# Causal attention: values projected per group of four heads in three rotating buffers, ten exponential slots in place of eight

## The chip, the cores and the metric

The kernel runs on one core of a Trainium2 chip. The metric is the device time of one execution in microseconds (us); the median of three runs of the kernel before is 2347.75 us (2345.16 to 2347.81). The engines are TensorE (PE in the profile, PEld for its weight loads), VectorE (DVE), ScalarE (ACT), GpSimd (POOL) and SyncE (SP, which here issues the DMAs).

## What is computed

A decoder layer for 4 batch elements of 1024 tokens and 512 channels: causal self-attention with 16 heads of 32 channels, cross-attention to 64 context tokens, a feed-forward part, and then a gated fusion that ends in a layer norm. All of it is float32. The change lies in the causal self-attention:

```python
xn1 = _ln(x, g1, be1)
q = jnp.einsum('btc,hcd->bhtd', xn, Wq) + bq[None, :, None, :]
k = jnp.einsum('bsc,hcd->bhsd', kv_src, Wk) + bk[None, :, None, :]
v = jnp.einsum('bsc,hcd->bhsd', kv_src, Wv) + bv[None, :, None, :]
scores = jnp.einsum('bhtd,bhsd->bhts', q, k) / scale      # scale = DH ** -0.5, so this multiplies
scores = jnp.where(mask[None, None], scores, -jnp.inf)
attn = jax.nn.softmax(scores, axis=-1)
out = jnp.einsum('bhts,bhsd->bhtd', attn, v)
```

## The kernel before, in words

The program has three stages: causal attention (1), cross-attention (2), feed-forward and fusion (3). Stage 1 runs over 16 groups g: batch element b = g // 4, four heads each. A group has two halves c2 (queries 0 to 511 and 512 to 1023); a half goes over key tiles j of 128 keys, 4 in the first half and 8 in the second, and over the four heads i.

The order of the work is written out by hand as a table of planned times: `order1` gives each step a number (1 unit is one group), sorts them, and every engine then walks the same list and takes the steps that are its own. An engine's queue is in order. `banks1` gives each step that needs PSUM one of seven banks, the eighth (`BO`) collects the attention output.

The steps that the change and the prediction touch:

- `lnT`, `lnh`, `lnl`: the layer norm of a batch element, transposed by PE (L722), split into a high part (`Q.xh`, ACT) and a low part (`Q.xl`, DVE). For b > 0 these stand in the third group of the batch element before.
- `pj`: projection of queries and keys of a group, `three` matmuls per k (L55, L56, L57: high by high, high by low, low by high), 512 columns each.
- `vm` and `ve`: projection of the values. One `vm` step is one k of one token tile st: `three` matmuls whose stationary operand is `Q.xh` or `Q.xl` (128 channels by 128 tokens) and whose moving operand is the whole row of `Wv`, 512 columns, so all 16 heads. Four k fill one PSUM bank, which `ve` (ACT, L873) copies to `Q.v[:, st, :]`. There are 8 st per batch element. For b = 0 they stand in the part ahead of group 0; for b > 0 in the second half of the last group of batch element b - 1, and `ve` waits until that group has read `Q.v[:, st, :]` for the last time (`s_pv`).
- `mx` (L745, DVE L1000 and L1004): the row maxima, from a matmul of their own.
- `sc` (L785), `low` (DVE L1011, the causal mask), `ex` (ACT L895): scores with keys on the partitions, and their exponentials. Tile j = 0 of a half goes to `Q.esum`, all others to a ring `Q.er` of 8 slots, `at % 8`. An `ex` waits until POOL has added the slot's former content into `esum` (`s_add`) and PE has multiplied it by the values (`s_pv`).
- `pv` (PE L797): four matmuls of exponentials by values, 32 output rows each, and on POOL the four additions into `esum` (L660). `fin` (L806) sums over the keys, `sao` (ACT L902) evicts the attention output of a half.

```python
def three(e, dst, lhs, rhs, start, stop):
    (lh, ll), (rh, rl) = lhs, rhs
    e.matmul(dst, lh, rh, start=start, stop=False)
    e.matmul(dst, lh, rl, start=False, stop=False)
    return e.matmul(dst, ll, rh, start=False, stop=stop)
```

`Q.v` is a tile of 8 rows of 512 elements per partition. Ahead of group 0 the same tile holds the tokens of batch element 0 (`x_rows`).

## Time and profile before

| | |
|---|---|
| median of three runs | 2347.75 us (2345.16 to 2347.81) |
| profiled execution | span 2338.9 us from the first to the last instruction |
| what lies around the span | 8.85 us, from the span to the median of the runs |
| stage 1, groups 0 to 15 | about 116 to 1033 us of the span |
| PE matmul / weight loads busy | 94% / 68% of the span |
| DVE / ACT / POOL busy | 60% / 37% / 40% of the span |

No time of the profiled execution beyond its span is listed, so the median stands for it. A matmul in the trace lasts longer than the distance to the next one, since matmuls are pipelined: what a matmul costs is read from start to start. A "busy" PE can still be waiting inside; idle time of PE is a lower bound on what it lacks.

### The profile page before, as it was taken

The page shows a single profiled execution, that of the slowest core. Times are in us where ns is not written, and L with a number is a line of the kernel's source. Part 1 is how long each engine was busy: PE and PEld are TensorE (multiplying, and loading weights), DVE is VectorE, ACT ScalarE, POOL GpSimd, SP SyncE. Part 2 cuts the span into 40 slices and gives each one's busy share as a digit, 9 for nine tenths or more (in the row PEclk, how much of TensorE's full clock was granted, in tenths as well). Part 3 has the DMA queues.
Part 4 walks back from the last instruction along what each step waited for, and adds up shares of the span by engine and source line. Part 5 has one row for each costly group of instructions (what it writes and reads, how often), then busy time and mean ns, then how long its engine had stood idle before and what let it go on. Part 6 is the DMA issues. An engine that isn't in the chain of part 4 may idle for free.

```text
span 2338.9 us, 31417 instructions
## 1 busy us (share of the span) xinstructions
PE 2198.0 (94%) x11206; PEld 1595.5 (68%) x11206; DVE 1410.1 (60%) x3349; ACT 868.2 (37%) x1598; POOL 933.6 (40%) x943
## 2 busy tenths in 40 slices
PE   7999999999999998789999998999999999999996
PEld 5655565556555654447777776788887887888784
DVE  5477757875786566735666668453455546454646
ACT  3155545654565455533443334321111122112213
POOL 1068657766777577773333333010111202011212
PEclk9999999999999998789999999999999999999998
DMA  7465545553556356212111121321112121212011
GB/s 231 55 93 97 92 71 77 103 93 62 83 97 97 60 88 124 69 56 85 59 55 55 59 95 55 113 86 36 50 54 75 52 82 44 87 55 68 33 36 50
DMA packets 106320, 177.29 MB, mean 76 GB/s; under 512 B 18334, under 2 KB 23454, under 8 KB 106160
## 3 DMA queue, kind: packets, MB, share of 16 engines
q1 hardware_dynamic: 106164, 175.29, 32.4%
q8 instruction: 88, 1.44, 0.3%
q14 instruction: 68, 0.56, 0.1%
HBM read 83.67 MB, written 40.13 MB: 53 GB/s over the span
## 4 chain that ended last, share of the span: by engine, by line
PE 75%; DVE 9%; issue 6%; ACT 4%; POOL 3%; DMA 2%; SPq 0%; POOLq 0%; ACTq 0%; DVEq 0%
PE psum L55 18%; PE psum L56 17%; PE psum L57 17%; PE psum L797 5%; PE psum L745 5%; PE psum L785 4%; PE psum L806 2%; DMA small<-es 2%; PE psum L703 1%; DVE psum L1000 1%; POOL es L660 1%; ACT sx L1346 1%; PE psum L1300 1%; DVE mx L1004 1%; PE psum L1292 1%
## 5 line engine op out<-in xcount | busy, mean ns | idle before, releaser
L660 POOL TENSOR_TENSOR es<-es,er 128x512 f32<-128x512 f32 (+3 forms) x640 | 589.6, 961 | 322.5 <-PE psum L797 283.4
L895 ACT ACTIVATE er<-psum 128x512 f32<-128x512 f32 (+3 forms) x640 | 280.4, 470 | 316.0 <-DVE psum L1011 181.2
L1000 DVE CUSTOM_DVE_ANT_0 psum<-psum,mask_ts 128x384 f32<-128x384 f32 (+3 forms) x512 | 247.9, 500 | 201.2 <-PE psum L745 200.5
L785 PE MATMUL psum<-qs,ks 100*128 100x512 f32 (+3 forms) x768 | 264.5, 377 | 17.1 <-DVE mx L1004 6.6
L745 PE MATMUL psum<-ks,qs 96*128 96x512 f32 (+3 forms) x768 | 267.2, 373 | 10.9 <-DVE mx L1000 6.6
L1850 ACT ACTIVATE fy<-psum,cols 128x512 f32<-128x512 f32 x128 | 88.2, 689 | 451.4 <-PE psum L57 450.9
L745 PEld LDWEIGHTS psum<-ks,qs 96*128 96x128 f32 x768 | 144.0, 194 | 109.7 <-issue 39.4
L1004 DVE TENSOR_REDUCE mx<-psum 128x1 fp32r<-128x512 f32 x256 | 175.1, 684 | 60.7 <-PE psum L745 59.8
L785 PEld LDWEIGHTS psum<-qs,ks 100*128 100x128 f32 x768 | 145.9, 196 | 92.4 <-DVE mx L1004 23.1
L55 PE MATMUL psum<-fh,hh 128*128 128x512 f32 x512 | 201.1, 393 | 7.1 <-DVE hl L1951 7.1
L55 PE MATMUL psum<-fah,fh 128*128 128x512 f32 x512 | 202.6, 396 | 0.0
L57 PE MATMUL psum<-fah,fl 128*128 128x512 f32 x512 | 199.8, 390 | 0.0
L56 PE MATMUL psum<-fal,fh 128*128 128x512 f32 x512 | 199.6, 390 | 0.0
L57 PE MATMUL psum<-fh,hl 128*128 128x512 f32 x512 | 199.4, 389 | 0.0
L56 PE MATMUL psum<-fl,hh 128*128 128x512 f32 x512 | 199.3, 389 | 0.0
L1949 DVE CAST hh<-fy 128x512 fp32r<-128x512 f32 x128 | 59.5, 465 | 228.8 <-ACT fy L1850 228.4
L1215 POOL TENSOR_TENSOR pp<-pp,small 128x1024 f32<-128x1024 f32 x32 | 61.2, 1913 | 266.7 <-DVE small L1481 266.7
L797 PE MATMUL psum<-er,v 128*32 128x512 f32 (+3 forms) x1280 | 152.3, 497 | 6.7 <-ACT er L895 6.2
L1746 POOL TENSOR_TENSOR et<-et,vpb 128x512 f32<-128x512 f32 x24 | 35.4, 1476 | 284.8 <-ACT et L1876 284.8
L1011 DVE TENSOR_TENSOR psum<-psum,mask_st 128x128 f32<-128x128 f32 x512 | 138.3, 303 | 15.0 <-PE psum L785 14.1
L55 PEld LDWEIGHTS psum<-fh,hh 128*128 128x128 f32 x512 | 96.1, 188 | 29.0 <-DVE hl L1951 9.5
L57 PEld LDWEIGHTS psum<-fah,fl 128*128 128x128 f32 x512 | 96.2, 188 | 20.5
(258 smaller groups left out, 4479.8 us busy)
## 6 DMA issues: line engine op xcount, KB each, us to landing
qs<-stage SPq DMA_DIRECT2D x96, 256.0 KB, 5.7
ks<-stage SPq DMA_DIRECT2D x96, 256.0 KB, 6.9
rs<-rs_d SPq DMA_DIRECT2D x32, 256.0 KB
sa_d<-rs SPq DMA_DIRECT2D x32, 256.0 KB, 2.2
sx<-sa_d SPq DMA_DIRECT2D x8, 1024.0 KB, 5.7
xt<-in_x SPq DMA_DIRECT2D x32, 256.0 KB, 6.1
x_d<-xt SPq DMA_DIRECT2D x32, 256.0 KB, 2.0
fw<-in_Wf SPq DMA_DIRECT2D x16, 512.0 KB, 5.3
```

The costliest lines, as they stand in the source:

```text
L55: e.matmul(dst, lh, rh, start=start, stop=False)
L56: e.matmul(dst, lh, rl, start=False, stop=False)
L57: return e.matmul(dst, ll, rh, start=False, stop=stop)
L660: e.tensor_tensor(es, es, er, ALU.add).then_inc(s_add.sem, 1)
L745: t = e.matmul(bank1(*s)[:, v * wd:v * wd + wd], Q.qs[par][0:96, i, 128 * ti:128 * ti + 128], Q.ks[par][0:96, i, c0:c0 + wd], start=True, ...
L785: t = e.matmul(ps[:, off:512], Q.ks[par][0:100, i, 128 * j:128 * j + 128], Q.qs[par][0:100, i, 512 * c2 + off:512 * c2 + 512], start=True, ...
L797: e.matmul(bank[BO][32 * i:32 * i + 32, off:512], Q.v[:, j, h:h + 32], src[:, off:512], start=j == 0, stop=j == nj - 1).then_inc(s_pv.sem, 1)
L895: e.activation(dst, bank1("sc", g, c2, j, i)[:, off:512], ACT.Exp, scale=SCALE).then_inc(s_freeS.sem, 1)
L1000: t = e.tensor_tensor_reduce(out=ps, in0=ps, in1=mask_ts[:, 512 - wd:512], scale=1.0, scalar=-3e38, op0=ALU.add, op1=ALU.max, accum_out=mx ...
L1004: e.tensor_reduce(mx[:, at:at + 1], bank1(*s)[:, 0:wd], AX, ALU.max).then_inc(s_red.sem, 1)
L1011: e.tensor_tensor(ps, ps, mask_st[:], ALU.add).then_inc(s_low.sem, 1)
L1850: e.activation(y[:], ring3(("h", c, m)), ACT.Relu, bias=col("bf1", m), scale=1.0).then_inc(s_r3.sem, 1)
```

## The change

The values are projected per group of four heads. A `vm` step is now one token tile i of one half hf of the key tokens (128 tokens), with all four k inside it: twelve matmuls whose moving operand is 128 columns of `Wv` in place of 512. Four such steps fill one bank, and one `ve` copies it. A group's values go to one of three buffers of two rows of `Q.v` each (`values(g)`); the two rows of `Q.v` that are left become slots 8 and 9 of the ring (`ring(at)`), and `ex` waits for the content of ten slots before.

The planned places: group 0 ahead of the attention; groups 1 and 2 of a batch element (g % 4) in the group before theirs; group 3 in the second half of group 1; group 0 of a batch element in the last group of the batch element before. So per batch element, 8 steps are hosted in its group 0, 16 in its group 1, none in its group 2, and 8 (of the next batch element) in its group 3.

```diff
@@ -144,13 +144,6 @@
         for qt in range(4):
             if b:
                 t += ln_times(b, qt, 4 * b - 2.5 if qt == 0 else 4 * b - 2.28 + 0.26 * qt, 4 * b - 2.05 + 0.25 * qt)
-        for st in range(8):
-            if b == 0:
-                s, d = at0(44 + 3.1 * st), 0.05
-            else:
-                s, d = 4 * b - 1 + cut + (1 - cut) * (st + 2.2) / 9, 0.057
-            t += spread(s, s + d, [(("vm", b, st, k), 1) for k in range(KT)])
-            t.append((s + d, ("ve", b, st)))
     for g in range(16):
         if g == 0:
             at = [at0(a) for a in (25, 30, 35, 40)]
@@ -166,6 +159,10 @@
                 t += proj_times(g, c2, wq, at[n], at[n] + (0.05 if g < 2 else 0.07 if g % 4 == 0 else 0.15))
                 back = (g - 2 + cut, g - 2 + cut + (1 - cut) * 0.54, g - 1, g - 1)[n] + 0.03
                 t.append((at[n] + 0.1 if g == 0 else max(at[n] + 0.22, back), ("stack", g, c2, wq)))
+        for hf in range(2):
+            s, d = (at0(52 + 8 * hf), 0.08) if g == 0 else (g - (1.45, 1.28)[hf], 0.1) if g % 4 == 3 else (g - (0.95, 0.5)[hf], 0.1)
+            t += spread(s, s + d, [(("vm", g, hf, i), 1) for i in range(4)])
+            t.append((s + d, ("ve", g, hf)))
         m0, m1, end = (at0(46), at0(54), cut - 0.12) if g == 0 else (0.25, 0.5, 0.97) if g == 1 else (g - 1.02, g - 0.72, g)
         t += spread(m0, m1, max_steps(g, 0)) + spread(m1, end, max_steps(g, 1))
         for c2, at in enumerate((m1, end)):
@@ -482,7 +479,7 @@
                 _, b, qt, kp = use
                 w.wait_ge(s_xl1, 8 * b + 2 * qt + kp + 1)
             elif use[0] == "vm":
-                w.wait_ge(s_v, 8 * use[1] + use[2] + 1)
+                w.wait_ge(s_v, 2 * use[1] + use[2] + 1)
             elif use[0] == "pj":
                 w.wait_ge(s_lo, Q.useP[use] + 1)
             elif use[0] == "mx":
@@ -510,6 +507,14 @@
             w.wait_ge(d_out0, 16 * 5)
             for j in range(2):
                 w.wait_ge(d_zm[j], 64)
+
+        def values(g):
+
+            return Q.v[:, 2 * (g % 3):2 * (g % 3) + 2, :].rearrange("p a (s n) -> p (a s) n", n=128)
+
+        def ring(at):
+
+            return Q.er[:, at % 10, :] if at % 10 < 8 else Q.v[:, at % 10 - 2, :]
 
         def x_rows(b, qt, i):
 
@@ -651,7 +656,7 @@
                     off = max(0, 128 * (j - 4 * c2))
                     for i in range(4):
                         at = Q.slot[g, c2, j, i]
-                        es, er = Q.esum[c2][i][:, off:512], Q.er[:, at % 8, off:512]
+                        es, er = Q.esum[c2][i][:, off:512], ring(at)[:, off:512]
                         if j == 1:
                             w.wait_ge(s_pv, Q.pv[g, c2, 0, i] + 1)
                         else:
@@ -759,15 +764,18 @@
                                      start=True, stop=True)
                     t.then_inc(s_fillM.sem, 1)
                 elif s[0] == "vm":
-                    _, b, st, k = s
-                    if k == 0:
+                    _, g, hf, i = s
+                    b, gg = divmod(g, 4)
+                    st = 4 * hf + i
+                    if i == 0:
                         free1(w, *s[:3])
                     w.wait_ge(s_wl1, 12)
-                    xn_ready(w, b, st // 2, k)
-                    ss = slice(128 * st, 128 * st + 128)
+                    ss, cs, to = slice(128 * st, 128 * st + 128), slice(128 * gg, 128 * gg + 128), slice(128 * i, 128 * i + 128)
                     Wh, Wl = Q.W["v"]
-                    t = three(e, bank1(*s[:3]), (Q.xh[:, k, ss], Q.xl[:, k, ss]), (Wh[:, k, :], Wl[:, k, :]), k == 0, k == 3)
-                    if k == 3:
+                    for k in range(KT):
+                        xn_ready(w, b, st // 2, k)
+                        t = three(e, bank1(*s[:3])[:, to], (Q.xh[:, k, ss], Q.xl[:, k, ss]), (Wh[:, k, cs], Wl[:, k, cs]), k == 0, k == 3)
+                    if i == 3:
                         t.then_inc(s_fillA.sem, 1)
                 elif s[0] == "sc":
                     _, g, c2, j, i = s
@@ -787,14 +795,13 @@
                     t.then_inc(s_fillS.sem, 1)
                 elif s[0] == "pv":
                     _, g, c2, j = s
-                    gg, nj, off = g % 4, 4 * c2 + 4, max(0, 128 * (j - 4 * c2))
+                    nj, off = 4 * c2 + 4, max(0, 128 * (j - 4 * c2))
                     for i in range(4):
                         w.wait_ge(s_freeS, Q.outS["sc", g, c2, j, i] + 1)
-                        w.wait_ge(s_v, 8 * (g // 4) + j + 1)
+                        w.wait_ge(s_v, 2 * g + j // 4 + 1)
                         w.wait_ge(s_sao, 2 * g + c2)
-                        src = Q.er[:, Q.slot[g, c2, j, i] % 8, :] if j else Q.esum[c2][i][:]
-                        h = 128 * gg + 32 * i
-                        e.matmul(bank[BO][32 * i:32 * i + 32, off:512], Q.v[:, j, h:h + 32], src[:, off:512],
+                        src = ring(Q.slot[g, c2, j, i]) if j else Q.esum[c2][i][:]
+                        e.matmul(bank[BO][32 * i:32 * i + 32, off:512], values(g)[:, j, 32 * i:32 * i + 32], src[:, off:512],
                                  start=j == 0, stop=j == nj - 1).then_inc(s_pv.sem, 1)
                 elif s[0] == "fin":
                     f = s[1]
@@ -842,7 +849,7 @@
                     w.wait_ge(s_fillA, u + 1)
                     if b:
                         w.wait_ge(s_fillJ, Q.useP["pj", 4 * b - 1, 1, 1] + 1)
-                        w.wait_ge(s_fillA, Q.useA["vm", b - 1, 7] + 1)
+                        w.wait_ge(s_fillA, Q.useA["vm", 4 * b - 1, 1] + 1)
                     e.activation(Q.xh[:, 2 * kp:2 * kp + 2, 256 * qt:256 * qt + 256], bank1("lnT", b, qt, kp).rearrange("p (k t) -> p k t", k=2),
                                  ACT.Copy).then_inc(s_xh1.sem, 1)
                 elif s[0] == "pjh":
@@ -865,12 +872,15 @@
                     e.activation(Q.qs[g % 2][96:100, 0, 512 * c2:512 * c2 + 512], bank1("mxT", g, c2)[96:100, :],
                                  ACT.Copy).then_inc(s_tq.sem, 1)
                 elif s[0] == "ve":
-                    _, b, st = s
-                    u = Q.useA["vm", b, st]
+                    _, g, hf = s
+                    u = Q.useA["vm", g, hf]
                     w.wait_ge(s_fillA, u + 1)
-                    if b:
-                        w.wait_ge(s_pv, Q.pv[4 * b - 1, 1, st, 3] + 1)
-                    e.activation(Q.v[:, st, :], bank1("vm", b, st), ACT.Copy).then_inc(s_v.sem, 1)
+                    if g >= 3:
+                        w.wait_ge(s_pv, Q.pv[g - 3, 1, 4 * hf + 3, 3] + 1)
+                    elif g == 2:
+                        w.wait_ge(s_fillA, Q.useA["lnT", 0, 2, 1] + 1)
+                    e.activation(values(g)[:, 4 * hf:4 * hf + 4, :], bank1("vm", g, hf).rearrange("p (s n) -> p s n", n=128),
+                                 ACT.Copy).then_inc(s_v.sem, 1)
                 elif s[0] == "ex":
                     _, g, c2, j, i = s
                     off, n = max(0, 128 * (j - 4 * c2)), 2 * g + c2
@@ -880,10 +890,12 @@
                         w.wait_ge(s_fillS, Q.useS["sc", g, c2, j, i] + 1)
                     if j:
                         at = Q.slot[g, c2, j, i]
-                        dst = Q.er[:, at % 8, off:512]
-                        if at >= 8:
-                            w.wait_ge(s_add, at - 7)
-                            w.wait_ge(s_pv, Q.pv[Q.slot_of[at - 8]] + 1)
+                        dst = ring(at)[:, off:512]
+                        if at >= 10:
+                            w.wait_ge(s_add, at - 9)
+                            w.wait_ge(s_pv, Q.pv[Q.slot_of[at - 10]] + 1)
+                        elif at >= 8:
+                            w.wait_ge(s_fillA, Q.useA["lnT", 0, 3, 1] + 1)
                         else:
                             w.wait_ge(s_wl1, 12)
                             w.wait_ge(s_bmm, 3)
```

DVE and SP have the same instructions in the same order before and after; POOL has the same additions in the same order, some of which read `v` in place of `er`.

Two places in PE's order follow. First PE in the second half of group 3, where batch element 1's values were projected all at once; in these rows `wvh,xh` and the like are the value projection, `xh,wqh` the query projection, `qs,ks` the scores, `ks,qs` the maxima, and the last number is the moving columns. Before:

```order
L785 MATMUL psum<-qs,ks 128x512
L745 MATMUL psum<-ks,qs 128x384
L55 MATMUL psum<-wvh,xh 128x512
L56 MATMUL psum<-wvl,xh 128x512
L57 MATMUL psum<-wvh,xl 128x512
L55 MATMUL psum<-xh,wqh 128x512
```

Now, in the same half of the same group:

```order
L793 MATMUL psum<-qs,ks 128x512
L750 MATMUL psum<-ks,qs 128x256
L55 MATMUL psum<-wvh,xh 128x128
L56 MATMUL psum<-wvl,xh 128x128
L57 MATMUL psum<-wvh,xl 128x128
```

A step of three matmuls of 512 columns (32 of them per batch element) became one of twelve matmuls of 128 columns (the last three rows are the first of its four triples), and this group has 8 of these steps where it had 32 of the others.

The second place is PE at the start of group 5, which had no value projection. Before:

```order
L745 MATMUL psum<-ks,qs 128x384
L785 MATMUL psum<-qs,ks 128x384
L55 MATMUL psum<-xh,wqh 128x512
L56 MATMUL psum<-xl,wqh 128x512
L57 MATMUL psum<-xh,wql 128x512
L797 MATMUL psum<-es,v 32x512 x4
```

Now:

```order
L55 MATMUL psum<-wvh,xh 128x128
L56 MATMUL psum<-wvl,xh 128x128
L57 MATMUL psum<-wvh,xl 128x128
L55 MATMUL psum<-xh,wqh 128x512
L56 MATMUL psum<-xl,wqh 128x512
L57 MATMUL psum<-xh,wql 128x512
L804 MATMUL psum<-es,v 32x512 x4
```

Ahead of the group's first `pv` there now stand steps of the value projection (the first three rows end one of them); group 5 has 16 of them in all, 192 matmuls.

## Rows read from the trace of the kernel before

**Rows 1.** The page: span, and busy time of PE's matmuls, its weight loads, DVE

```profile
span 2338.9 us, 31417 instructions
PE 2198.0 (94%) x11206; PEld 1595.5 (68%) x11206; DVE 1410.1 (60%) x3349; ACT 868.2 (37%) x1598; POOL 933.6 (40%) x943
```

**Rows 2.** The page: the chain that ended last, by engine

```profile
PE 75%; DVE 9%; issue 6%; ACT 4%; POOL 3%; DMA 2%; SPq 0%; POOLq 0%; ACTq 0%; DVEq 0%
```

**Rows 3.** Windows by group: us, length, busy by engine, PE clock, DMA

```profile
64.00:116.00 52.00, 52.00 (x231) 35.72 (x231) 23.75 (x73) 8.47 (x16) 0.00 (x0) 1.00 0.34 46
116.00:168.00 52.00, 50.37 (x280) 30.85 (x280) 42.10 (x139) 27.27 (x58) 37.69 (x41) 1.00 0.61 88
168.00:220.00 52.00, 49.51 (x277) 29.05 (x277) 39.37 (x130) 29.46 (x63) 37.51 (x40) 0.97 0.53 81
...
345.00:395.00 50.00, 48.70 (x277) 29.69 (x277) 35.62 (x120) 27.88 (x59) 35.00 (x35) 1.00 0.45 68
395.00:447.00 52.00, 48.42 (x274) 28.61 (x273) 39.33 (x127) 29.11 (x62) 40.33 (x46) 1.00 0.59 93
447.00:504.00 57.00, 52.31 (x290) 30.98 (x289) 43.82 (x144) 35.21 (x71) 41.20 (x48) 0.97 0.54 104
504.00:571.00 67.00, 65.71 (x348) 43.06 (x347) 36.74 (x122) 31.00 (x65) 43.48 (x50) 1.00 0.49 78
571.00:621.00 50.00, 48.70 (x277) 29.67 (x276) 35.70 (x119) 27.88 (x60) 34.58 (x35) 1.00 0.45 69
621.00:675.00 54.00, 52.06 (x277) 30.97 (x275) 39.60 (x122) 29.43 (x63) 40.95 (x47) 0.91 0.57 90
...
800.00:850.00 50.00, 48.69 (x277) 29.68 (x277) 35.61 (x121) 27.83 (x59) 35.23 (x36) 1.00 0.44 68
850.00:899.00 49.00, 46.53 (x261) 27.20 (x260) 35.22 (x119) 26.91 (x58) 38.16 (x42) 1.00 0.57 88
899.00:966.00 67.00, 54.79 (x246) 30.01 (x245) 49.88 (x124) 29.38 (x63) 47.42 (x53) 0.74 0.55 127
```

**Rows 4.** Timeline of PE in group 3: start us, us, instruction

```profile
301.98 0.40 PE L55 MATMUL psum<-wvh,xh 128*128 128x512 f32 x1
302.21 0.40 PE L56 MATMUL psum<-wvl,xh 128*128 128x512 f32 x1
302.45 0.39 PE L57 MATMUL psum<-wvh,xl 128*128 128x512 f32 x1
302.68 0.40 PE L785 MATMUL psum<-qs,ks 100*128 100x512 f32 x1
```

**Rows 5.** Timeline of PE ahead of group 0, four matmuls of 128 columns

```profile
64.92 0.56 PE L745 MATMUL psum<-ks,qs 96*128 96x128 f32 x4
65.32 0.45 PE L55 MATMUL psum<-wvh,xh 128*128 128x512 f32 x1
65.60 0.39 PE L56 MATMUL psum<-wvl,xh 128*128 128x512 f32 x1
```

**Rows 6.** Timeline of PE ahead of group 0, one matmul of 128 columns

```profile
95.99 0.22 PE L745 MATMUL psum<-ks,qs 96*128 96x128 f32 x1
96.05 0.46 PE L55 MATMUL psum<-wvh,xh 128*128 128x512 f32 x1
```

**Rows 7.** Waits between 116 and 1030 us: us in total, times, longest us

```profile
ACT v L873 <- PE psum L57: 17.7, 15, 2.8
ACT er L895 <- POOL es L660: 14.7, 23, 0.9
ACT er L895 <- PE psum L797: 8.6, 11, 0.9
PE psum L797 <- ACT er L895: 5.9, 14, 0.6
ACT v L873 <- PE psum L797: 3.8, 3, 1.3
```

**Rows 8.** Groups by line: the eviction of the values

```profile
L873 ACT ACTIVATE v<-psum 128x512 f32<-128x512 f32 x32 | 19.1, 598 | 58.3 <-PE psum L57 54.5 <-PE psum L797 3.8
```

## The prediction

> **What bounds the kernel now.** I read the page first. PE's matmuls are busy for 94% of the span, its weight loads for 68%, the next engine, DVE, for 60% [rows 1]; the chain that ended last is PE for 75% of its length [rows 2]. A busy matmul row can hide waits, so the second view is the windows cut at the ends of the groups [rows 3]. In batch element 1, group 4 (345 to 395) takes 50 us and PE lacks 1.3 us of it; group 5 (395 to 447) takes 52 and lacks 3.6; group 6 (447 to 504), which holds the layer norm of the next batch element, takes 57 and lacks 4.7; group 7 (504 to 571), with all the values of the next batch element, takes 67 and lacks 1.3. So the groups without a layer norm are bound by PE: what is added to PE there lengthens them, and what is taken away shortens them, as long as DVE (35.2 to 42.1 us busy in them) stays below. The part ahead of group 0 (64 to 116) is PE from end to end, 52.00 of 52. The last two groups are another matter: group 14 (899 to 966) takes 67 us with PE busy 54.8 at a clock of 0.74 [rows 3].
>
> The third view is the distance from one matmul to the next, since that, not its duration, is what PE pays. A wide triple of the value projection goes from 301.98 to 302.68, 0.70 us, 0.23 for each of 512 columns [rows 4]. Four matmuls of 128 columns in a row, each with its own weight load of 128 columns, go from 64.92 to 65.32, 0.40 us, and the matmul behind them then needs 0.28 to its successor where 0.23 is usual [rows 5]. One lone matmul of 128 columns between bigger ones needs 0.06 [rows 6]. I read this so: the first of a run has its weights loaded beside the matmul before, so it pays only its 0.06; the other three pay (0.40 - 0.06) / 3 = 0.113 each, which must be the weight load, since the columns alone take 0.06; and the one behind pays 0.05 for its own load.
>
> **The change part by part.** *The matmuls.* Columns in all are the same, but a matmul of a quarter of the columns costs half, not a quarter. A new step is a run of twelve: 0.06 + 11 x 0.113 + 0.05 = 1.35 us. Before, the same work was three wide matmuls, 0.70 us. There are 128 steps before (32 per batch element) and 128 now, so PE gets 128 x (1.35 - 0.70) = 83.2 us more. Spread over the stage, with 22.4 us (32 x 0.70) for a batch element before, and 10.8 us (8 x 1.35) for a group now:
> - ahead of group 0: -22.4 + 10.8 = -11.6;
> - groups 3, 7, 11, which end in the first steps of 4, 8, 12: -11.6 each, -34.8;
> - groups 0, 4, 8, 12 host one following group: +10.8 each, +43.2;
> - groups 1, 5, 9, 13 host two: +21.6 each, +86.4.
>
> The sum is +83.2 again. The levelling therefore gives nothing by itself: the giving and the taking groups are both bound by PE.
>
> Bounds of the price: at most 1.35, as the rows have it; at least 0.40 / 4 = 0.10 for each of a run [rows 5], which makes 1.20 a step and +64 in all. I take 1.35, since a run of twelve is nearer to the three that paid in full than to the first.
>
> *What PE's idle time takes in.* In the eight groups that get work, PE lacked 1.6, 2.5, 1.3, 3.6, 1.3, 1.9, 1.3 and 2.5 us [rows 3], 16.0 in all. These are waits for DVE, ACT and POOL, which run on while PE projects values, so most of it should go: I take -12, between 0 and -16. Of the clock: group 9 had a mean of 0.91, group 1 0.97, of the two levels 1.2 and 2.4 GHz, after waits of PE; full speed would give back at most 54 x 0.09 + 52 x 0.03 = 6.5 us. I take -2.
>
> *The ring.* With ten slots an `ex` waits less for a slot. In the whole stage ACT waited 14.7 us for POOL's additions and 8.6 for PE's products of the slot before, never over 0.9 at a time, while PE waited for an exponential for 5.9 us in all [rows 7]. Since PE sets the end, the ring can give no more than 5.9; I take -1, as half of these waits can come from the mask and the scores just as well.
>
> *The evictions of the values.* 32 copies of 0.60 us before [rows 8], 32 of as many elements now. Before, three of them waited 3.8 us for the group that still read the tile [rows 7]; a buffer is now free since two groups. They stand in ACT's queue where the last step is due, and the exponentials behind them wait too. ACT waited 17.7 us in 15 such places before [rows 7] without PE lacking it. The bound is 32 x 0.60 = 19 us if each eviction's time were added to PE's path; the other end is -3.8. I take 0, because between the last step of a half and the first product that needs an exponential behind the eviction the order has other scores, maxima and projections, and ACT is busy for little more than half of these groups [rows 3].
>
> *The rest.* SP's and DVE's orders don't change, so no DMA moves past another; POOL adds the same tiles. The layer norm of the next batch element now also waits for the last value steps of group 3, but these stand ahead of it in PE's queue, so this costs nothing. Group 2, which holds the layer norm, hosts none; groups 14 and 15 neither.
>
> **The sum.** 83.2 - 12 - 2 - 1 = +68. The span of the profile is 2338.9, 8.85 less than the median of 2347.75; I add to the median: **2416 us**. The ends: 64 - 16 - 6.5 - 5.9 - 3.8 = +32 (2380), and 83.2 + 19 = +102 (2450).
>
> **The rivals.**
> - *Weights loaded partly beside the run.* If in a run of twelve the loads overlap better than in a run of four, a matmul costs between 0.06 [rows 6] and 0.113 [rows 5], at the middle 0.086: 1.04 a step, 128 x 0.34 = +43.5, less 15 for idle time and clock, 2376. Against it: the three that paid in full stand behind each other in one run, and nothing in a longer run gives the load more cover. 9%. The Trainium skill (page "TensorE: Matmul & The Clock Gate", section "Back-to-back issue gap") says that a stream of weight load and matmul pairs settles at some 81 ns each for 128 columns. By it a step would be 0.97 and the sum +35 before idle time, as an estimate; the trace has 0.113 for just such pairs, so the measurement decides.
> - *Faster.* If the loads were hidden wholly, each matmul would cost 0.06 as the lone one does [rows 6]: 0.72 a step, +2.6 in all, so the levelling and the ring come through: 2.6 - 16.0 - 6.5 - 5.9 = -26, 2322. It decides below some 0.072 us per matmul, where 128 x (12 x 0.072 - 0.70) equals the 21 that idle time and half of the rest give back. Against it stand the 0.40 of four [rows 5]; for it only that a lone one has cover. 4%. The same section's formula for a single matmul, columns by the clock plus 2.5 ns, gives 56 ns and would speak for this case; the run of four contradicts it here.
> - *A new wait.* The evictions block ACT, PE gets its exponentials later by one eviction each time: +19, so 2435. Against it is ACT's share of time. 8%.
> - *Nothing is levelled or absorbed.* If the idle times of PE stay where they are, since they belong to chains of DVE and ACT that shift along with PE, the sum is +83: 2431. 14%.
>
> **How the numbers follow.** My forecast has 65%, the rivals 9, 4, 8 and 14. All but the second are slower. The range is 2380 to 2440: from the forecast's own low end, with the cheapest run and all that idle time, clock and ring can give, up to the unabsorbed sum and the new wait. It leaves out the second rival, most of the first, and the forecast's and the new wait's upper end, together about 2 in 10. A measurement of this kernel can tell about 0.2% (4.7 us) from no change. Slower by more has 94%: every case but the second, less a little for a smaller price together with all idle time taken in; faster by more has 4%, within it 2%.
>
> **What would show it.** Lines 55 to 57 on `wvh` and `wvl` should each have 512 matmuls of 128 columns, and a run of twelve should last about 1.35 us from its first start to the start behind it. Groups 1, 5, 9 and 13 should take 68 to 73 us, groups 4, 8 and 12 about 58, groups 3, 7 and 11 about 58, group 2 and the last two as before; the attention should begin some 11 us earlier. PE should lack less than 2 us in the groups that got work, and ACT's waits for POOL and for `pv` should nearly vanish without the time following. I am wrong if a run of twelve takes under 1.1 us, or if groups 1 and 5 stay under 64 us.

## The result and the profile after

The changed kernel takes 2397.7 us (median of 4 runs, 2390.9 to 2400.2) against 2346.5 for the kernel before (4 runs, 2344.5 to 2347.8): ratio 1.0211, 95% interval 1.0193 to 1.0229, so 51 us slower. A second series of 5 runs gave 2394.7 against 2346.5, 1.0211 again [1.0197, 1.0225]. The forecast was 2416, 68 us slower, range 2380 to 2440. One execution, in run 7 below, took 2469.1 us at a mean clock of 0.839 where the others of its kernel have 0.979 to 0.982; it is left out of the figures.

The profiled execution after took 2400.15 us, its span 2398.3, so 1.85 us lie around a span. With as much around it, the profiled execution before was at 2340.8, 5.7 us under its median, and the one after is 2.5 us above its own; that is why the spans lie 59.4 us apart and the medians 51.2.

The page of the changed kernel, busy time and the chain that ended last by engine, to [rows 1, 2]:

```profile
span 2398.3 us, 33698 instructions
PE 2266.0 (94%) x12358; PEld 1696.7 (71%) x12358; DVE 1410.0 (59%) x3349; ACT 863.2 (36%) x1598; POOL 934.3 (39%) x943
...
PE 78%; DVE 8%; issue 4%; ACT 4%; DMA 3%; POOL 2%; SPq 1%; POOLq 0%; DVEq 0%; ACTq 0%
```

PE has 1152 matmuls more with as many weight loads, DVE's busy time is unchanged, and PE's share of the chain rose from 75 to 78%.

The timeline of PE in group 4 of the changed kernel, around one step of the value projection, to [rows 4, 5]:

```profile
361.69 0.22 PE L55 MATMUL psum<-wvh,xh 128*128 128x128 f32 x1
361.75 0.28 PE L56 MATMUL psum<-wvl,xh 128*128 128x128 f32 x1
361.87 0.28 PE L57 MATMUL psum<-wvh,xl 128*128 128x128 f32 x1
...
362.87 0.28 PE L57 MATMUL psum<-wvh,xl 128*128 128x128 f32 x1
362.98 0.39 PE L793 MATMUL psum<-qs,ks 100*128 100x384 f32 x1
363.21 0.34 PE L750 MATMUL psum<-ks,qs 96*128 96x384 f32 x1
363.39 0.34 PE L793 MATMUL psum<-qs,ks 100*128 100x384 f32 x1
```

The first narrow matmul is followed after 0.06 us, the others after 0.11, and twelve take 1.29 us. The matmul of 384 columns behind them is followed after 0.23 where the next of 384 columns takes 0.18. That makes 1.34 us for a step, 1.35 in the forecast. The Trainium skill (page "TensorE: Matmul & The Clock Gate", section "LDWEIGHTS (loading the stationary operand)") puts a weight load at its columns over 1.2 GHz; as an estimate from that, 107 ns for 128. The 0.11 us of these rows agrees with it. The 81 ns of the Trainium skill (same page, section "Back-to-back issue gap"), which was weighed ahead of the run, is not what this trace shows.

The windows cut at the groups' ends in the changed kernel, to [rows 3]; columns are the window, its length, busy time of PE, PEld, DVE, ACT and POOL with the number of instructions, PE's clock, the DMA share and GB/s:

```profile
63.00:115.00 52.00, 52.00 (x272) 37.04 (x271) 26.96 (x83) 7.42 (x13) 0.00 (x0) 0.90 0.45 57
115.00:172.00 57.00, 55.26 (x342) 37.61 (x341) 39.18 (x129) 26.08 (x56) 38.02 (x41) 1.00 0.48 72
172.00:241.00 69.00, 68.28 (x470) 50.66 (x469) 39.16 (x130) 31.67 (x67) 40.17 (x44) 1.00 0.41 62
...
355.00:412.00 57.00, 56.41 (x363) 38.62 (x363) 36.43 (x121) 28.44 (x61) 39.42 (x43) 1.00 0.50 77
412.00:481.00 69.00, 68.05 (x468) 50.32 (x466) 39.30 (x132) 31.25 (x67) 42.00 (x49) 1.00 0.43 64
481.00:537.00 56.00, 50.70 (x285) 30.20 (x285) 43.03 (x142) 34.07 (x71) 35.62 (x39) 0.97 0.57 105
537.00:595.00 58.00, 57.30 (x364) 39.10 (x364) 36.74 (x123) 28.68 (x61) 43.45 (x48) 1.00 0.51 84
...
652.00:721.00 69.00, 67.77 (x465) 49.91 (x463) 39.30 (x132) 31.46 (x66) 41.48 (x48) 1.00 0.42 63
...
891.00:959.00 68.00, 67.05 (x460) 49.63 (x460) 36.88 (x123) 29.63 (x63) 40.82 (x47) 1.00 0.43 69
```

Groups 1, 5, 9 and 13 grew from 52, 52, 54 and 49 us to 69, 69, 69 and 68; group 4 from 50 to 57; group 7 shrank from 67 to 58; group 6 stayed at 56 to 57. The giving and the taking groups are where the forecast had them, and in the eight groups that got work PE lacks 0.6 to 1.7 us, less than 2 as forecast. Group 14, forecast to stay, fell from 67 us to 63 (959 to 1022) without a change of its work. Ahead of group 0 the forecast does not hold: the attention's first eviction (tile `sao`) starts at 132.3 us where it was 133.3, 1 us earlier and not 11, and the clock of the first row is 0.90 where it was 1.00.

ACT's waits in the changed kernel between 115 and 1090 us, to [rows 7]:

```profile
ACT er L907 <- PE psum L804: 8.6, 10, 0.9
...
ACT er L907 <- POOL es L665: 2.1, 3, 1.0
ACT v L907 <- POOL es L665: 1.4, 2, 0.7
```

ACT waited 14.7 us for POOL before, and now 3.5 in all. (`v L907` are exponentials that go to the two new slots.) Its waits for PE's products were to nearly vanish too, and did not: 8.6 us before and 8.6 now.

### The profile page after: what moved, and what is told of

Same layout as the page of the kernel before. It is cut to its first block, busy times and chain, and to the rows that moved or that the text cites. A ratio compares the mean times of both kernels' runs of the same rounds, so it can differ in the third digit from the quotient of the medians.

```text
span 2398.3 us, 33698 instructions
## 1 busy us (share of the span) xinstructions
PE 2266.0 (94%) x12358; PEld 1696.7 (71%) x12358; DVE 1410.0 (59%) x3349; ACT 863.2 (36%) x1598; POOL 934.3 (39%) x943
## 4 chain that ended last, share of the span: by engine, by line
PE 78%; DVE 8%; issue 4%; ACT 4%; DMA 3%; POOL 2%; SPq 1%; POOLq 0%; DVEq 0%; ACTq 0%
PE psum L55 19%; PE psum L57 18%; PE psum L56 18%; PE psum L750 5%; PE psum L804 5%; PE psum L793 5%; DMA small<-es 2%; PE psum L708 1%; PE psum L813 1%; DVE psum L1012 1%; ACT sx L1358 1%; PE psum L1312 1%; DVE mx L1016 1%; PE psum L1253 1%; PE psum L1304 1%
## 5 line engine op out<-in xcount | busy, mean ns | idle before, releaser
L665 POOL TENSOR_TENSOR es<-es,er 128x512 f32<-128x512 f32 (+3 forms) x512 | 493.0, 992 | 345.1 <-PE psum L804 304.3
L907 ACT ACTIVATE er<-psum 128x512 f32<-128x512 f32 (+3 forms) x512 | 230.8, 484 | 282.6 <-DVE psum L1023 165.8
L793 PE MATMUL psum<-qs,ks 100*128 100x512 f32 (+3 forms) x768 | 259.1, 373 | 12.0 <-DVE mx L1016 2.9
L1023 DVE TENSOR_TENSOR psum<-psum,mask_st 128x128 f32<-128x128 f32 x512 | 139.3, 304 | 20.8 <-PE psum L793 20.3
L56 PE MATMUL psum<-wvl,xh 128*128 128x128 f32 x512 | 141.6, 277 | 0.0
L57 PE MATMUL psum<-wvh,xl 128*128 128x128 f32 x512 | 141.6, 277 | 0.0
L804 PE MATMUL psum<-er,v 128*32 128x512 f32 (+3 forms) x1024 | 136.2, 506 | 0.4
```

The lines of the kernel that those rows point to most:

```text
L665: e.tensor_tensor(es, es, er, ALU.add).then_inc(s_add.sem, 1)
L793: t = e.matmul(ps[:, off:512], Q.ks[par][0:100, i, 128 * j:128 * j + 128], Q.qs[par][0:100, i, 512 * c2 + off:512 * c2 + 512], start=True, ...
L804: e.matmul(bank[BO][32 * i:32 * i + 32, off:512], values(g)[:, j, 32 * i:32 * i + 32], src[:, off:512], start=j == 0, stop=j == nj - 1).th ...
L907: e.activation(dst, bank1("sc", g, c2, j, i)[:, off:512], ACT.Exp, scale=SCALE).then_inc(s_freeS.sem, 1)
L1023: e.tensor_tensor(ps, ps, mask_st[:], ALU.add).then_inc(s_low.sem, 1)
```

## The experiments

Two theories stood at the start. **W**: PE pays the weight load of every narrow matmul, and the rest of the change matters little. **P**: the new places, buffers and evictions cost the time, and the narrow matmuls hide in waits. **R**, that the ring pays back much of the loss, was the third.

**1. The narrow matmuls alone**, in the kernel before:

```diff
...
-                    t = three(e, bank1(*s[:3]), (Q.xh[:, k, ss], Q.xl[:, k, ss]), (Wh[:, k, :], Wl[:, k, :]), k == 0, k == 3)
+                    for kk in range(KT):
+                        xn_ready(w, b, st // 2, kk)
+                        t = three(e, bank1(*s[:3])[:, cs], (Q.xh[:, kk, ss], Q.xl[:, kk, ss]), (Wh[:, kk, cs], Wl[:, kk, cs]), kk == 0, kk == 3)
```

> The kernel before, with the values still projected by batch element, in the same places, tile and ring; only each group of four wide matmuls is cut into matmuls of 128 columns (a step is twelve of them, one quarter of the columns, all four k). Theory W (the weight load of each narrow matmul is what PE pays): 128 steps at 1.29 + 0.05 us in place of 0.70 us is +82 us of PE work, all of it ahead of group 0 and in groups 3, 7 and 11, where PE lacked 1.3 us or less: about +78, 2424 us, more than the whole change, since nothing is levelled. Theory P (the places and the buffers of the change cost the time, narrow matmuls hide in waits): within 15 us of the kernel before, under 2362 us.

Measured: 2442.0 us, ratio 1.0396 [1.0366, 1.0425], +96. P falls. It is even 18 us more than W said, in runs that lie 20 us apart (2426.9 to 2446.9). Group 3 in the kernel before, then this run's windows ahead of group 0 and in group 3:

```profile
277.00:345.00 68.00, 66.70 (x353) 43.93 (x352) 37.42 (x127) 31.67 (x66) 44.01 (x51) 1.00 0.49 78
...
64.00:148.00 84.00, 84.00 (x505) 68.30 (x504) 24.05 (x73) 8.36 (x16) 0.00 (x0) 0.86 0.20 28
310.00:395.00 85.00, 83.71 (x601) 65.63 (x600) 37.00 (x124) 31.02 (x65) 43.57 (x50) 1.00 0.42 66
```

Group 3 grew from 68 to 85. The part ahead of group 0 grew from 52 to 84 us, by 32 where 8 x 4 x 0.64 = 20 were to come: there the clock is 0.86. Of the two levels, 1.2 and 2.4 GHz, 0.86 means 28% of 84 us at the lower, which is 12 us lost; PE was busy all the time. These 12 are most of the 18; the other 6 are not traced.

**2. Wide enough matmuls, by pairs of groups.** The change's idea with two groups at a time and 256 columns, two buffers of four rows, eight slots (the steps' index is now a pair p, half steps of two k):

```diff
-            return Q.v[:, 2 * (g % 3):2 * (g % 3) + 2, :].rearrange("p a (s n) -> p (a s) n", n=128)
+            return Q.v[:, 4 * (p % 2):4 * (p % 2) + 4, :].rearrange("p a (s n) -> p (a s) n", n=256)
...
-                    for k in range(KT):
+                    for k in range(2 * (i % 2), 2 * (i % 2) + 2):
```

> The changed kernel with the values projected by two groups at a time (eight heads, 256 columns a matmul), two rotating buffers, ring of eight slots; hosted in groups 0 and 1 (for groups 2 and 3 of the batch element) and in group 3 (for the next batch element), 12 matmuls of 256 columns per token tile. Theory W: 256 columns cost 0.12 us start to start, so the load is covered; PE gets 384 x 2 x 0.12 = 92 us for 89 before, and the levelled work takes in idle time of groups 0 and 1: faster than before by 5 to 20 us, 2326 to 2341 us. Theory P: values by group of heads cost by their places and waits, so 20 to 50 us slower than before.

Measured: 2325.4 us, 0.9905 [0.9890, 0.9920], 20 us faster than before and 0.6 below W's range. W holds. The timeline of its PE in group 3:

```profile
279.85 0.28 PE L55 MATMUL psum<-wvh,xh 128*128 128x256 f32 x1
279.96 0.28 PE L56 MATMUL psum<-wvl,xh 128*128 128x256 f32 x1
280.08 0.28 PE L57 MATMUL psum<-wvh,xl 128*128 128x256 f32 x1
```

Twice the columns of a narrow matmul take 0.12 us, as good as the same.

**3. The ring put back to eight slots**, in the changed kernel:

```diff
-            return Q.er[:, at % 10, :] if at % 10 < 8 else Q.v[:, at % 10 - 2, :]
+            return Q.er[:, at % 8, :]
...
-                        if at >= 10:
-                            w.wait_ge(s_add, at - 9)
-                            w.wait_ge(s_pv, Q.pv[Q.slot_of[at - 10]] + 1)
...
+                        if at >= 8:
+                            w.wait_ge(s_add, at - 7)
+                            w.wait_ge(s_pv, Q.pv[Q.slot_of[at - 8]] + 1)
```

> The changed kernel with the ring put back to eight slots; all else as changed. Theory W says that the ring gives PE at most the 5.9 us it waited for exponentials: 2396 to 2404 us, no different from the changed kernel or a few us slower. Theory R (ten slots paid for part of the narrow matmuls, which is why the loss is 51 and not 82): 2412 us or more, with ACT waiting for POOL and for products again by some 20 us and PE behind it.

Measured: 2423.5 us, 1.0321 [1.0301, 1.0340], 26 us slower than the change. This is R's number, not W's. ACT's waits in its trace are back at those of the kernel before, as R said, but PE is not behind them: in its products it waited for exponentials of the ring for 2.7 us, where it was 5.9 in the kernel before [rows 7].

```profile
ACT er L905 <- POOL es L665: 16.1, 24, 0.9
...
ACT er L905 <- PE psum L804: 9.3, 11, 0.9
...
PE psum L804 <- ACT er L905: 2.7, 5, 0.5
```

The windows show where the time went: the first 21 us of groups 3, 7 and 11 of this kernel.

```profile
296.00:317.00 21.00, 21.00 (x88) 16.39 (x88) 6.05 (x30) 6.12 (x12) 4.76 (x10) 0.51 0.62 90
546.00:567.00 21.00, 21.00 (x90) 16.70 (x89) 6.12 (x28) 5.70 (x11) 4.81 (x9) 0.53 0.64 90
795.00:816.00 21.00, 20.99 (x147) 15.36 (x147) 13.82 (x58) 10.40 (x24) 13.01 (x21) 1.00 0.65 93
```

All three begin at the same place of their group's order, and PE is busy throughout. In the first two it runs at half clock and gets through 88 and 90 matmuls, in the third at full clock through 147. Mean clocks of the runs say the same: 0.963 to 0.971 in the four runs with eight slots, 0.976 to 0.979 in the four of the change. In the profiled pair (0.971 of 2412.7 us, 0.976 of 2398.3) the lower clock is worth 2412.7 x 0.029 - 2398.3 x 0.024 = 12.4 us of the 14.4 between the spans; over all four runs of each, with mean clocks of 0.967 and 0.978, about 27 us, as much as the whole difference. The clock fell here at the end of group 2, where PE waited:

```profile
294.00:298.00 4.00, 3.02 (x13) 2.25 (x13) 3.00 (x16) 1.83 (x5) 4.00 (x6) 0.75 0.21 77
298.00:302.00 4.00, 4.00 (x21) 3.90 (x19) 1.12 (x6) 2.17 (x4) 2.61 (x6) 0.50 1.09 155
```

So a theory **C** took R's place: a short wait at the end of the layer-norm group lets the clock fall, and the runs of narrow matmuls behind it keep it low. Two of PE's waits there are for exponentials, 0.55 us each; in the change there is one, and its clock stayed at 1.00 from 295 to 303, though PE was busy for 6.81 of those 8 us.

**4. Two of three products**: the changed kernel's value projection without the product of the tokens' low part and the weights' high part.

```diff
-                        t = three(e, bank1(*s[:3])[:, to], (Q.xh[:, k, ss], Q.xl[:, k, ss]), (Wh[:, k, cs], Wl[:, k, cs]), k == 0, k == 3)
+                        e.matmul(bank1(*s[:3])[:, to], Q.xh[:, k, ss], Wh[:, k, cs], start=k == 0, stop=False)
+                        t = e.matmul(bank1(*s[:3])[:, to], Q.xh[:, k, ss], Wl[:, k, cs], start=False, stop=k == 3)
```

> The changed kernel with one of three products of the value projection left out (tokens low by weights high), so twelve narrow matmuls become eight in each of the 128 steps. Theory W: 128 x 4 x 0.112 = 57 us less PE work; if the groups that host values are bound by PE all through, the time falls by 45 to 57 us, to about 2341 to 2353; the idle time that the values had taken in comes back in part. Theory P: the waits stay, so it falls by less than 25 us, above 2373.

Measured: 2344.0 us, 54 us less than the change, for 57 us less of PE work. The hosts are bound by PE all through.

**5 and 6. The whole change but the narrowness, with ten and with eight slots.** Three buffers of one group each, as in the change, but neighbouring groups projected together in 256 columns, in the odd group before them (groups 1 and 3 of a batch element; its groups 0 and 2 host nothing), and evicted by two copies:

```diff
...
+                    for gg in range(2):
+                        e.activation(values(2 * p + gg)[:, 2 * hf:2 * hf + 2, :],
+                                     bank1("vm", p, hf).rearrange("p (s a n) -> p s a n", a=2, n=128)[:, :, gg, :],
+                                     ACT.Copy).then_inc(s_v.sem, 1)
...
```

> All of the change (three rotating buffers of one group each, ten slots, values by group) except the narrow matmuls: two neighbouring groups are projected together in matmuls of 256 columns and evicted into two buffers, in the odd group before them. Theory W (the loss is the weight load of matmuls too narrow to cover it): PE is back at about 92 us for the values, so 2310 to 2330 us, faster than before by 15 to 35. Theory P (the buffers and places cost): slower than before, over 2350 us.

> The same with eight slots. Theory C (with narrow matmuls the two more slots were worth 26 us because a short wait of PE let its clock fall to half and runs of narrow matmuls kept it there for 20 us; the waits themselves are short): with 256 columns no such long stretches at 1.2 GHz, so 0 to 6 us slower than with ten slots. Theory R (two more slots save PE some 25 us of waits in any case): 18 to 30 us slower than with ten slots.

Measured: 2323.3 us with ten slots, 0.9908 [0.9892, 0.9923]; 2326.2 with eight, 0.9913 [0.9899, 0.9927]. Between them is no difference that can be told, though ACT waited 17.9 us for POOL with eight and 4.7 with ten. So the 25 us of R are not there: C, not R. And the change without its narrow matmuls is 24 us faster than before; the narrow matmuls cost it 2397.7 - 2323.3 = 74 us. The places differ too, but run 2, with other places and buffers at 256 columns, is within 2 us of run 5.

**7. Half of the values that group 3 hosts (a quarter of the next batch element's) moved into the layer-norm group**, in the version of run 2, the rest moved earlier within group 3:

```diff
-                    s, d = g - (0.95, 0.7, 0.45, 0.2)[hf], 0.1
+                    s, d = g - (1.6, 1.35, 0.85, 0.45)[hf], 0.1
```

> The version with pairs of groups, two buffers and eight slots, with half of the next batch element's values moved from its last group into the third, where the layer norm leaves PE idle for 4 to 5 us of 57. Theory W with levelling: those 5.8 us leave a group bound by PE and go where about 4 us are idle, three times over: 5 to 12 us faster than the same kernel without the move. Rival: the third group is bound by the chain of the layer norm on DVE and ACT, into which the steps cut, so it grows by as much: within 4 us.

Measured: 2327.1 us (four runs, 2325.5 to 2330.4), 0.9915 [0.9900, 0.9931]: no gain, the rival's side. Group 2 takes 63 us where it took 57, and group 3, 54 for 57: the layer-norm group, though PE is idle in it, gave back all that group 3 won.

**8 and 9. The narrow runs moved away from the wait**, with eight slots, and the change once more beside it:

```diff
-            s, d = (at0(52 + 8 * hf), 0.08) if g == 0 else (g - (1.45, 1.28)[hf], 0.1) if g % 4 == 3 else (g - (0.95, 0.5)[hf], 0.1)
+            s, d = (at0(52 + 8 * hf), 0.08) if g == 0 else (g - (1.45, 1.28)[hf], 0.1) if g % 4 == 3 else (g - ((0.95, 0.5), (0.7, 0.35))[g % 4 == 0][hf], 0.1)
```

> The changed kernel with eight slots again, and the first half of the next batch element's values moved from the start of groups 3, 7 and 11 (a twentieth into the group) to a third into it, the second half to two thirds. PE's work, the ring and the tiles are those of the version with eight slots. Theory C (a wait at the end of the layer-norm group lets the clock fall, and the narrow runs right behind it keep it at 1.2 GHz for 20 us): the first matmuls of these groups are now scores, maxima and projections of 256 to 512 columns, so the stretches at half clock get short, and the time falls by 12 to 25 us, to 2399 to 2412 us. Theory R (the slots' waits themselves cost 26 us): within 6 us of 2423.

> The changed kernel as it is, on the same chip as the run beside it. Both theories: 2390 to 2400 us. Theory C: the mean clock stays at 0.976 to 0.980 where that of the version with eight slots was 0.963 to 0.971, and if its trace shows a stretch at half clock of over 7 us in this stage, the matmuls in it are narrow ones or have a few columns.

Measured: 2405.3 us, 1.0255 [1.0241, 1.0269], 18 us faster than run 3 with the same slots, tiles and work: that the runs of narrow matmuls behind the fall were the loss is shown, the second half of C. That the wait starts the fall is read from the rows and was not tried by itself. The first 21 us of groups 3 and 7 here:

```profile
297.00:318.00 21.00, 20.94 (x119) 13.37 (x117) 13.77 (x56) 9.07 (x21) 13.39 (x21) 0.84 0.71 105
...
543.00:564.00 21.00, 20.99 (x120) 13.58 (x119) 13.19 (x54) 8.90 (x22) 12.61 (x20) 0.84 0.76 109
```

The clock still falls, but is back sooner. The change again gave 2394.7 us, so 10.6 are left between eight and ten slots. Of the 14.8 between the two profiled spans the mean clocks, 0.975 and 0.979, are worth 2406.8 x 0.025 - 2392.0 x 0.021 = 9.9; what the rest is, no run separates. One part of the last expectation missed: in its trace the longest stretches at half clock lie in groups 14 and 15 (clock 0.80 and 0.90), where there are no values to project and PE waits for DVE.

## Why the prediction held, and where it was off

**The price of the narrow matmul** was the term on which all rested, and it was right: 1.34 us a step for 1.35. That the stream of the moving columns does not set the distance is shown by run 2, in which 256 columns cost no more than 128. That it is the load, and not a least distance of any two matmuls, is seen ahead of group 0 of the changed kernel, in matmuls with one moving column:

```profile
73.59 1.05 PE L717 MATMUL psum<-cols,er 128*128 128x1 f32 x8
74.50 0.48 PE L750 MATMUL psum<-ks,qs 96*128 96x512 f32 x1
...
78.07 0.34 PE L708 MATMUL psum<-cols,vcol 128*4 128x1 f32 x8
78.34 0.50 PE L750 MATMUL psum<-ks,qs 96*128 96x512 f32 x1
```

Eight with weights of 128 columns take 0.91 us, 0.114 each; eight with weights of 4 columns take 0.27, 0.034 each.

**Where it falls.** Groups 1, 5, 9 and 13 were to take 68 to 73 and took 68 to 69; groups 4 and 7, about 58, took 57 and 58; the layer-norm group stayed. Run 4 confirms that in the changed kernel these groups are bound by PE to the last few us. The attention was to begin 11 us earlier: the 11.6 us less work ahead of group 0 are there, but four steps of group 1's values, 4 x 1.34 = 5.4 us, stand ahead of the first eviction, which the forecast overlooked, and 5 us went to the clock (below).

**What does not reach the time** was sized at 15 us for idle time, clock and ring together, and is more; but part of it was lost again ahead of group 0 and at the end. The windows of the two profiled executions, cut at the ends of groups 0, 2, 6, 10 and 14 (each window from the second on holds whole groups), show it. The kernel before:

```profile
0.00:168.20 168.20, 152.59 (x741) 101.56 (x742) 97.02 (x283) 59.54 (x110) 44.49 (x62) 1.00 0.60 126
168.20:277.40 109.20, 101.05 (x562) 59.52 (x561) 83.32 (x272) 64.23 (x133) 77.38 (x85) 0.97 0.53 93
277.40:503.80 226.40, 215.52 (x1186) 132.66 (x1185) 155.59 (x510) 123.50 (x256) 159.95 (x177) 0.99 0.52 86
503.80:732.20 228.40, 219.49 (x1186) 134.97 (x1185) 156.62 (x511) 123.33 (x257) 160.01 (x177) 0.96 0.51 85
732.20:966.10 233.90, 216.63 (x1131) 130.70 (x1131) 157.88 (x485) 115.50 (x244) 164.50 (x178) 0.93 0.51 92
966.10:2338.90 1372.80, 1292.69 (x6410) 1036.12 (x6408) 759.68 (x1298) 382.10 (x600) 327.30 (x268) 0.98 0.18 62
```

The changed kernel:

```profile
0.00:172.20 172.20, 156.44 (x837) 109.50 (x838) 97.33 (x283) 57.27 (x106) 44.71 (x62) 0.96 0.59 123
172.20:297.40 125.20, 119.06 (x754) 80.89 (x753) 83.06 (x272) 65.96 (x137) 75.72 (x83) 0.99 0.48 81
297.40:537.50 240.10, 232.22 (x1474) 157.88 (x1473) 154.39 (x504) 121.97 (x256) 160.57 (x178) 0.99 0.50 81
537.50:777.00 239.50, 232.00 (x1474) 157.53 (x1473) 155.03 (x511) 122.00 (x257) 159.99 (x177) 0.99 0.49 81
777.00:1021.70 244.70, 231.20 (x1419) 153.75 (x1419) 160.28 (x490) 114.64 (x244) 165.93 (x179) 0.94 0.49 88
1021.70:2398.30 1376.60, 1295.12 (x6410) 1037.17 (x6408) 759.93 (x1298) 381.39 (x600) 327.39 (x268) 0.98 0.18 62
```

| stretch | matmul work added | time added | difference |
|---|---|---|---|
| to the end of group 0 | -11.6 + 10.8 = -0.8 | +4.0 | +4.8 |
| groups 1, 2 | +21.6 | +16.0 | -5.6 |
| groups 3 to 6 | -11.6 + 10.8 + 21.6 = +20.8 | +13.7 | -7.1 |
| groups 7 to 10 | +20.8 | +11.1 | -9.7 |
| groups 11 to 14 | +20.8 | +10.8 | -10.0 |
| the rest | 0 | +3.8 | +3.8 |
| sum | +83.2 | +59.4 | -23.8 |

From group 1 to group 14, 32.4 us of the added work did not become time, against the 15 of the forecast. The clock is worth some 10 of them, by clocks rounded to 0.01: length times what the clock lacks of 1, before and after, gives 2.0 in groups 1 and 2, 6.7 in groups 7 to 10 (228.4 x 0.04 - 239.5 x 0.01) and 1.7 in groups 11 to 14, next to nothing in groups 3 to 6. The other 22 stand where the forecast had 12 for PE's waits and a bound of 16. The rows of these windows leave 45.2 us of groups 1 to 14 without a matmul before and 35.0 after, so 10.2 of the 22 show as idle time of PE; 12 do not. The step that failed there is the equation of what PE lacks with what the busy rows leave open: a matmul is drawn with 0.27 us or more where the next starts after 0.11 to 0.23, so a wait shorter than the rest of its bar doesn't show. That the 12 are such waits is what is left over, not something a row shows. And 4 of the 32.4 lie in group 14 (67 to 63 us), which got no work, for a reason that no run gives. Run 4 bears the size out: its value projection is 83 - 57 = 26 us more work than in the kernel before, and its 2344.0 us are no more than that kernel takes, so the first 26 us cost nothing and the next 57 cost 54.

With 12 + 2 + 1 replaced by 32.4, and the +8.6 of the first and the last stretch, the sum is the 59.4 of the spans. Of the +3.8 of the last stretch, where no values are projected, 0.9 lie in group 15 and 2.9 behind it. From 1530 to 1550 the clock is 0.91 where it was 1.00 at about the same place before (1472 to 1492), worth 20 x 0.09 = 1.8 us; the rest stays unexplained. The two errors, 17.4 too little taken in and 8.6 without a term, have opposite signs, and that the first was half cancelled by the second is luck. The medians are 8 us closer than the spans: 5.7 us come from the profiled execution before, which was that much under its median, and 2.5 from the one after.

**The ring** was sized at 1 us, and removing it cost 26. Its direct worth was small, as forecast: with 256 columns it is 2.9 us between the medians of runs 5 and 6, which is within their scatter. What I had not seen is that in the change as it stands the clock stays up with it: 18 of the 26 came back in run 8 by moving narrow runs alone. The 5.9 us of PE's waits that I took as the bound bound only the waits, not what comes behind them.

**The clock** I had giving back 2 us at no more than 6.5. It gave back more in the groups, as above (group 9's went from 0.91 to 1.00), and took away ahead of group 0, where the forecast had no term for it: 52 x 0.10 = 5 us, about the +4.8 of the first stretch. The runs speak for the narrow ones as the cause: from 66 to 116 us the clock is 0.76 to 0.93 in all six traces with value matmuls of 128 columns (the change twice, runs 1, 3, 4 and 8), and 1.00 in the other five (the kernel before, runs 2, 5, 6 and 7).

**The rivals.** Loads partly hidden: excluded by the timeline. Loads wholly hidden: likewise, and my case for it was thin; the lone matmul of [rows 6] pays 0.06, but the one behind it, from 96.05 to the next at 96.34, pays the other 0.06, so lone and grouped narrow matmuls cost about the same. Nothing absorbed: wrong, as above. Evictions that block ACT: run 4 leaves no room for 19 us of them, since taking out 57 us of PE's work gave 54. Two small sums of the prediction are off without moving it: the bound on the clock, 54 x 0.09 + 52 x 0.03, is 6.4 and not 6.5, and 16.0 with half of the clock's and the ring's bounds is 22 and not 21.

**By runs.** The change against run 5, which differs in the width, the places that go with pairs of groups and two copies for one, is 74 us; 128 steps at 1.34 against 6 x 0.12 = 0.72 are 79. The mean clocks of the two are alike (0.976 to 0.980 over nine runs of the change, 0.976 to 0.982 over four of run 5), so the clock doesn't explain the 5 us between; places and short waits may, and no run separates them.

## What to carry to other kernels

Cutting a matmul's moving side below what covers its weight load was paid in full here once PE's waits were used up: 512 columns cost 0.23 us, 256 cost 0.12, and 128 cost 0.11. When work is to be cut finer for levelling or to free buffers, cut it only down to the width at which the stream still covers the load (256 columns here); the version of run 5 keeps the three buffers and ten slots at 256 columns and is 24 us faster than the kernel before, 74 faster than the change. And a term "at most the waits that the profile shows" holds only as long as the clock behind those waits stays the same, which run 3 shows can fail.

## What the runs showed that was not expected

The clock fell, and stayed down, while PE was busy without a gap. Ahead of group 0 in the changed kernel, behind sixteen matmuls of one moving column, the timeline of PE and the window of these 12 us:

```profile
79.75 0.27 PE L57 MATMUL psum<-wvh,xl 128*128 128x128 f32 x1
79.86 0.28 PE L55 MATMUL psum<-wvh,xh 128*128 128x128 f32 x1
...
80.57 0.42 PE L57 MATMUL psum<-wvh,xl 128*128 128x128 f32 x1
80.79 0.41 PE L55 MATMUL psum<-wvh,xh 128*128 128x128 f32 x1
```

```profile
80.00:92.00 12.00, 12.00 (x40) 6.62 (x38) 2.10 (x6) 1.19 (x2) 0.00 (x0) 0.57 0.02 5
```

The distance goes from 0.11 to 0.21-0.22 us in the middle of one run: at 1.2 GHz it doubles, though it is the weight load that sets it. (5.7 of the 12 us are eight matmuls with weights of a single column.) Behind the fall at the start of groups 3 and 7 PE stayed there for about 20 us when runs of matmuls of 128 columns came first (0.51 and 0.53 over 21 us, run 3); with wider matmuls first it was mostly at 2.4 GHz in the same stretch (0.84 in both, run 8). At the lower clock 88 matmuls took the time of 147. So the narrow matmuls of this kernel cost twice: their loads, and up to 10 us where the clock fell ahead of them (21 x 0.49, run 3). What makes the clock fall and brings it back, the runs do not tell.
